# Feed-forward weights prepared in chunks inside the attention loop, and feed-forward tiles two deep

## The reference

```
q = layernorm(x) @ Wq;  k = ctx @ Wk;  v = ctx @ Wv        # 16 heads of 128
q, k = rmsnorm(q) * gq, rmsnorm(k) * gk                    # over the 128 of a head
x = x + tanh(g_xattn) * (softmax(q k^T / sqrt(128)) v) @ Wo

def weight_quant(w):                       # one scale for the whole matrix
    scale = max(mean(|w|), 1e-5);  return clip(round(w / scale), -1, 1) * scale
def act_quant(x):                          # one scale for each row
    scale = 127 / max(max|x|, 1e-5);  return clip(round(x * scale), -128, 127) / scale
def bitlinear(x, w): return act_quant(x) @ weight_quant(w)^T

n = layernorm(x)
x = x + tanh(g_ffn) * bitlinear(silu(bitlinear(n, w_gate)) * bitlinear(n, w_up), w_down)
```

## Time and profile before

| what | value |
|---|---|
| median of 3 runs (lowest, highest) | 2481.73 us (2481.36, 2483.34) |
| the profiled execution's own time | 2482.65 us |
| its span, first to last instruction | 2480.5 us, mean granted TensorE clock 0.97 |
| last product of attention, last residual | ends 2090.8 us, 2092.0 us |
| feed-forward block starts, first gate product | 2094.97 us, 2174.41 us |
| last store issued | 2478.1 us |

### The profile page before, as it was taken

One profiled execution on the slowest core, in us unless ns is written; L12 is line 12 of the kernel. 1 busy time (PEld: TensorE's weight loads), 2 busy tenths in 40 slices (PEclk: granted clock), 3 DMA queues, 4 the chain that ended last, 5 costly groups with the idle time before them and its releaser, 6 DMA issues. The chain is left out here.

```text
span 2480.5 us, 52473 instructions
## 1 busy us (share of the span) xinstructions
PE 2256.4 (91%) x16482; PEld 1597.2 (64%) x16634; DVE 1903.3 (77%) x4175; ACT 1577.8 (64%) x3226; POOL 1200.9 (48%) x1538
## 2 busy tenths in 40 slices
PE   2599999999999999999999999999999995589998
PEld 1377777777677767677767777777777773344443
DVE  4588878877878787877787788778887773589996
ACT  3567666766666666666666676667676763744443
POOL 4365646565656565656565656565656551000000
PEclk8799999999999999999999999999999998799999
DMA  6466666666666656666666666666666653434443
GB/s 199 103 112 113 122 111 119 113 121 112 116 116 121 107 118 116 122 112 116 114 122 113 116 112 123 113 115 113 124 113 118 115 113 106 160 77 106 118 114 93
DMA packets 887466, 289.31 MB, mean 117 GB/s; under 512 B 847760, under 2 KB 859312, under 8 KB 886704
## 3 DMA queue, kind: packets, MB, share of 16 engines
q1 hardware_dynamic: 887216, 286.15, 60.0%
HBM read 63.21 MB, written 13.11 MB: 31 GB/s over the span
## 5 line engine op out<-in xcount | busy, mean ns | idle before, releaser
L747 DVE TENSOR_TENSOR khat<-keys_ps,krs 128x512 f32<-128x512 f32 (+1 forms) x384 | 263.4, 686 | 289.9 <-POOL krs L989 289.9
L995 POOL TENSOR_TENSOR ksplit<-khat,ksplit 128x512 bf16<-128x512 f32 (+1 forms) x384 | 444.0, 1158 | 59.8 <-ACT ksplit L549 59.1
L986 POOL TENSOR_SCALAR kvar<-kss 128x4 f32<-128x4 f32 (+1 forms) x384 | 86.2, 225 | 674.0 <-DVE kss L737 674.0
L989 POOL TENSOR_TENSOR krs<-kvar,minus_half 128x4 f32<-128x4 f32 (+1 forms) x384 | 387.0, 1008 | 32.0
L569 ACT ACTIVATE early<-score_ps,nbias,qrs 100x361 f32<-100x361 f32 x512 | 330.5, 651 | 91.0 <-DVE nbias L765 88.5
L578 ACT ACTIVATE psplit<-early,rden 100x361 bf16<-100x361 f32 x512 | 304.9, 596 | 83.0 <-DVE rden L771 81.5
L554 ACT ACTIVATE ksq<-keys_ps 128x512 f32<-128x512 f32 (+1 forms) x384 | 228.6, 596 | 202.4 <-PE keys_ps L25 201.1
L777 DVE SCALAR_TENSOR_TENSOR psplit<-early,rden,psplit 100x361 bf16<-100x361 f32 x512 | 323.1, 641 | 7.8 <-ACT psplit L578 3.7
L549 ACT ACTIVATE ksplit<-khat 128x512 bf16<-128x512 f32 (+1 forms) x384 | 240.2, 625 | 115.5 <-DVE khat L747 105.0
L23 PE MATMUL keys_ps<-wk_hi,ctxT 128*128 128x512 bf16 (+1 forms) x649 | 249.8, 385 | 62.0 <-DVE khat L747 40.6
L755 DVE TENSOR_REDUCE nmax<-score_ps 100x1 f32<-100x361 f32 x512 | 269.1, 526 | 45.9 <-PE score_ps L25 45.9
(11 more groups left out here) (155 smaller groups left out, 5295.6 us busy)
## 6 DMA issues: line engine op xcount, KB each, us to landing
ctx_raw<-in_ctx SPq DMA_DIRECT2D x31, 256.0 KB, 3.0
xin<-in_x SPq DMA_DIRECT2D x32, 200.0 KB
xres<-in_x SPq DMA_DIRECT2D x32, 200.0 KB
x_rows<-xres SPq DMA_DIRECT2D x32, 200.0 KB
xin<-x_rows SPq DMA_DIRECT2D x25, 256.0 KB, 2.8
xres<-x_rows SPq DMA_DIRECT2D x25, 256.0 KB, 2.6
out<-xres SPq DMA_DIRECT2D x25, 256.0 KB, 2.9
kT<-ksplit SPq DMA_TRANSPOSE x384, 3.1
```

Of the source, the lines that this page charges most:

```text
L747: dve.tensor_tensor(khat[0:KV[t], k, :].rearrange("p (h d) -> p h d", h=G), keys_ps[k][0:KV[t], :].rearrange("p (h d) -> p h d", h=G), rs, ...
L989: pool.tensor_tensor(krs[0:KV[t], k, :], kvar[0:KV[t], k, :], minus_half[0:KV[t], 0:G], ALU.pow).then_inc(krs_done, 1)
L995: pool.tensor_tensor(ksplit[0:KV[t], t, 1, :], khat[0:KV[t], (u + t) % 2, :], ksplit[0:KV[t], t, 0, :], ALU.subtract).then_inc(k_lo_done, 1)
```

## The change

The host lays the three feed-forward weights out turned, as one array of 3 x 128 rows of 8192 f32 (w_ffn): row p of a matrix holds what partition p needs. A matrix is handled in 16 chunks of 512 columns, one in each of the 16 turns of a loop body. The loop of seven passes becomes: pairs 0 and 1 as straight code, a loop of three passes (one for each matrix) with a sum chunk in every turn, a loop of three passes with a chunk to be made ternary in every turn, and pairs 14 and 15 as before. In the first kind SP loads a chunk and ACT sums the absolute values; at the end of the pass DVE adds the 16 sums and SP stores them as a row of 128. In the second kind DVE first finds the scale from that row; each chunk is loaded again, scaled and rounded (one DVE instruction), clipped (a second), taken to bf16 by POOL and stored to DRAM (w_tern). In the last pair SP loads w_tern into the place of Wq's and Wk's parts, when these have been read for the last time. yT now shares its place with qsq.

The feed-forward block begins with x, reads only the stored sums, and runs two tiles deep: gate and up of tile t + 2 before down of tile t, statistics and quantising of x four tiles ahead. The quantised x goes through ACT's cast and a DMA transpose in place of PE's. The hidden rows are quantised by ACT in two halves and turned in two halves. A Silu at the start of the block comes before the tanh.

The attention part:

```diff
+    MATRICES, W_COLS = w_ffn.shape[0] // P, w_ffn.shape[1]
+    CHUNKS = BODY * UNITS
+    CHUNK = W_COLS // CHUNKS
+    SUM_LOOPS = (1, 1 + MATRICES)
+    TERN_LOOPS = (1 + MATRICES, 1 + 2 * MATRICES)
+    assert TERN_LOOPS[1] < PAIRS // BODY
...
+        w_raw, w_out = sb("w_raw", [P, CHUNK], F32), sb("w_out", [P, CHUNK], BF16)
+        w_abs, w_abs1 = sb("w_abs", [P, CHUNKS], F32), sb("w_abs1", [P, 1], F32)
+        w_part, w_tot = sb("w_part", [P, P], F32), sb("w_tot", [P, 1], F32)
+        w_scale, w_inv = sb("w_scale", [P, 1], F32), sb("w_inv", [P, 1], F32)
...
+            def load_chunk(j, i, u, k, job):
+                if job == "sum":
+                    sp.wait_ge(w_summed, chunk(i, u) + 1)
+                    sp.sem_inc(sp_passed, 1)
+                else:
+                    sp.wait_ge(w_rounded, tern_chunk(i, u) + 1)
+                    sp.sem_inc(sp_passed, 1)
+                sp.dma_start(w_raw[:, :], w_ffn[w_rows(j, job), k * CHUNK:(k + 1) * CHUNK]).then_inc(w_raw_in, 16)
+                if job == "tern" and k == 0:
+                    m = j - TERN_LOOPS[0]
+                    sp.wait_ge(w_inv_done, m + 1)
+                    sp.sem_inc(sp_passed, 1)
+                    sp.dma_start(w_part[:, :], w_sums[bass.ds(m, 1), :].partition_broadcast(P)).then_inc(w_part_in, 16)
+            def store_chunk(j, i, u, k, job):
+                if job == "tern":
+                    sp.wait_ge(w_rounded, tern_chunk(i, u) + 2)
+                    sp.sem_inc(sp_passed, 1)
+                    sp.dma_start(w_tern[w_rows(j, job), k * CHUNK:(k + 1) * CHUNK], w_out[:, :]).then_inc(w_tern_out, 16)
+                elif k == CHUNKS - 1:
+                    m = j - SUM_LOOPS[0]
+                    sp.wait_ge(w_abs_read, m + 2)
+                    sp.sem_inc(sp_passed, 1)
+                    sp.dma_start(w_sums[bass.ds(m, 1), :].rearrange("a p -> p a"), w_abs1[:, :]).then_inc(w_sums_out, 16)
+            def load_ternary(u):
+                gate_up = wq_split[:, :, :, :].rearrange("p a c n -> p a (c n)")
+                down = wk_split[:, :, :, :].rearrange("p a c n -> p (a c n)")
+                if u == 4:
+                    sp.wait_ge(w_tern_out, (MATRICES * CHUNKS + 1) * 16)
+                    sp.wait_ge(shared_done, use(PAIRS - 1, ("q", UNITS - 5, QD - 1))[0] + 1)
+                for m, part, parts in {4: ((0, 0, 4),), 5: ((0, 1, 4),), 6: ((0, 2, 4), (0, 3, 4), (1, 0, 4)),
+                                       7: ((1, 1, 4), (1, 2, 4), (1, 3, 4)), 8: ((2, 0, 2), (2, 1, 2))}.get(u, ()):
+                    if m == 2 and part == 0:
+                        sp.wait_ge(keys_done, tile(PAIRS - 1, UNITS - 1, KVT - 1) + 1)
+                    cols = slice(part * (W_COLS // parts), (part + 1) * (W_COLS // parts))
+                    dst = gate_up[:, m, cols] if m < 2 else down[:, cols]
+                    sp.dma_start(dst, w_tern[m * P:(m + 1) * P, cols]).then_inc(w_tern_in, 16)
...
+            def turn(i, u, last, par, j=None, job=None):
+                if job is not None:
+                    load_chunk(j, i, u, par * UNITS + u - 1, job)
...
+                    store_chunk(j, i, u, par * UNITS + u - 1, job)
+                if last:
+                    load_ternary(u)
...
+            for i in range(SUM_LOOPS[0] * BODY):
+                for u in range(1, UNITS + 1):
+                    turn(i, u, False, i % BODY)
+            with sp.Fori(*SUM_LOOPS) as j:
                 for r in range(BODY):
                     for u in range(1, UNITS + 1):
-                        turn(j * BODY + r, u, False, r)
-            for i in range(LOOPS * BODY, PAIRS):
+                        turn(j * BODY + r, u, False, r, j, "sum")
+            sp.wait_ge(w_sums_out, (MATRICES + 1) * 16)
+            sp.wait_ge(w_summed, MATRICES * CHUNKS + 1)
+            with sp.Fori(*TERN_LOOPS) as j:
+                for r in range(BODY):
+                    for u in range(1, UNITS + 1):
...
+            def sum_chunk(j, i, u, k):
+                eng.wait_ge(w_raw_in, (chunk(i, u) + 1) * 16)
+                if k == 0:
+                    eng.wait_ge(w_abs_read, j - SUM_LOOPS[0] + 1)
+                act.activation(w_raw[:, :], w_raw[:, :], ACT.Abs, accum_out=w_abs[:, k:k + 1]).then_inc(w_summed, 1)
...
+            def clip_chunk(j, i, u, k):
+                n = tern_chunk(i, u)
+                eng.wait_ge(w_raw_in, (chunk(i, u) + 1) * 16)
+                if k == 0:
+                    eng.wait_ge(w_inv_done, j - TERN_LOOPS[0] + 2)
+                dve.tensor_scalar(w_raw[:, :], w_raw[:, :], w_inv[:, 0:1], ROUND, ALU.mult, ALU.add).then_inc(w_scaled, 1)
+                eng.wait_ge(w_scaled, n + 1)
+                dve.tensor_scalar(w_raw[:, :], w_raw[:, :], ROUND + 1.0, ROUND - 1.0,
+                                  ALU.min, ALU.max).then_inc(w_clipped, 1)
...
+                    clip_chunk(j, i, u, par * UNITS + u - 1)
                     scale_keys(i, v + 2, 0)
...
                     scale_keys(i, v + 2, 1), scale_keys(i, v + 2, 2)
+                if job == "tern":
+                    clip_chunk(j, i, v, par * UNITS + v - 1)
...
+            def round_chunk(j, i, u, k):
+                n = tern_chunk(i, u)
+                eng.wait_ge(w_clipped, n + 1)
+                eng.sem_inc(pool_passed, 1)
+                eng.wait_ge(w_tern_out, n * 16 + 16)
+                eng.sem_inc(pool_passed, 1)
+                pool.tensor_scalar(w_out[:, :], w_raw[:, :], -ROUND, 1.0, ALU.add, ALU.mult).then_inc(w_rounded, 1)
...
                     query_scale(i, u)
+                if job == "tern":
+                    round_chunk(j, i, u, par * UNITS + u - 1)
                     key_scale(i, v + 2, 1), keys_lo(i, v + 2, 0)
...
                     keys_lo(i, v + 2, 1), keys_lo(i, v + 2, 2)
+                if job == "tern":
+                    round_chunk(j, i, v, par * UNITS + v - 1)
...
```

The feed-forward part (the steps of SP, PE, ACT and DVE) and the host's:

```diff
+            def step(t, s, ahead):
+                if ahead >= 5 or not isinstance(t, int):
+                    load_x(t + 5, 1 - s)
+                if ahead >= 1:
+                    turn_hidden(t + 1, 1 - s, 0)
+                if ahead >= 3:
+                    turn_x(t + 3, 1 - s)
+                if ahead >= 1:
+                    load_residual(t + 1, 1 - s)
+                    turn_hidden(t + 1, 1 - s, 1)
                 sp.wait_ge(res_done, t + 2)
                 sp.dma_start(out[bass.ds(t * P, P), :], xres[:, s, :]).then_inc(out_done[s], 16)
...
+            def step(t, s, ahead):
+                if ahead >= 2:
+                    gate_up(t + 2, s)
                 down(t, s)
...
+            def quantise(t, s, a):
+                cols = slice(a * HALF, (a + 1) * HALF)
+                eng.wait_ge(hinv_done, t + 1)
+                act.activation(hid[:, s, cols], hid[:, s, cols], ACT.Copy, bias=ROUND,
+                               scale=hinv[:, s:s + 1]).then_inc(hq_done, 1)
...
+            def step(t, s, ahead):
+                if ahead >= 2:
+                    gated(t + 2, s, 0)
+                if ahead >= 1:
+                    quantise(t + 1, 1 - s, 0)
+                if ahead >= 2:
+                    gated(t + 2, s, 1)
+                if ahead >= 1:
+                    cast_hidden(t + 1, 1 - s, 0)
+                if ahead >= 3:
+                    cast_x(t + 3, 1 - s)
+                if ahead >= 2:
+                    gated(t + 2, s, 2)
+                if ahead >= 1:
+                    quantise(t + 1, 1 - s, 1)
+                if ahead >= 2:
+                    gated(t + 2, s, 3)
+                if ahead >= 1:
+                    cast_hidden(t + 1, 1 - s, 1)
...
-                dve.tensor_scalar(hid[:, s, :], hid[:, s, :], hinv[:, 0:1], ROUND,
-                                  ALU.mult, ALU.add).then_inc(hq_done, 1)
...
+            def step(t, s, ahead):
+                if ahead >= 4:
+                    x_stats(t + 4, s)
+                down_scale(t, s)
+                if ahead >= 2:
+                    hidden(t + 2, s)
+                    hidden_scale(t + 2, s)
+                if ahead >= 4:
+                    x_quant(t + 4, s)
                 residual(t, s)
...
+    w = np.concatenate([inputs[n].T.reshape(-1, 128, inputs[n].shape[0]).transpose(1, 0, 2).reshape(128, -1)
+                        for n in _FFN])
```

More of the change, by code:

```diff
@@ L534, in _ @@
             first_turn(-1, UNITS)
-            with eng.Fori(0, LOOPS) as j:
-                for r in range(BODY):
-                    for u in range(1, UNITS, 2):
-                        two_turns(j * BODY + r, u, False, r)
-            for i in range(LOOPS * BODY, PAIRS):
+            for i in range(SUM_LOOPS[0] * BODY):
+                for u in range(1, UNITS, 2):
+                    two_turns(i, u, False, i % BODY)
+            for loops, job in ((SUM_LOOPS, "sum"), (TERN_LOOPS, "tern")):
+                with eng.Fori(*loops) as j:
+                    for r in range(BODY):
+                        for u in range(1, UNITS, 2):
```

(47 more changed lines are left out.)

382 lines of the change are left out of this document (173 added, 209 removed).

## The result

The changed kernel takes 2463.1 us (median of 4 runs, 2459.8 to 2469.8), the one before 2482.5 beside it: ratio 0.9925, 95% interval 0.9907 to 0.9944. The forecast was 2405.5 and the range ended at 2440. The sign was right, and most of the gain is missing: 19 us came, 76 were forecast. The profiled execution took 2469.8 us, the longest of the four; its span is 2468.0.

A forecast was written before the change was run, and what follows sets the result against it. PE was taken to bound the attention loop, with DVE and PE both nearly full in the feed-forward tiles. From 2482.65 us, -68 - 32 + 24 = -76 gave 2406.6, median 2405.5; range 2380 to 2440, own range 2390 to 2420.

The forecast's parts named there:

- Part 1, the hole: Feed-forward start: weight summing, rounding and transposes leave, so the first gate product comes some 11 us in: -68 us.
- part 2, the tiles: Feed-forward tiles: DVE loses work, PE becomes the bound at 10.4 us a tile instead of 11.67: -32 us.
- the DVE-bound rival: Feed-forward tiles stay DVE's, period 11.2 us, not 10.4: 18 us more, 2424 us; chance 0.12.
- Jumps back: Attention loop: four jumps at body ends instead of six, 3.1 us each: -6 us.
- Part 3, clips: Attention loop: DVE's clips delay PE, 28 us; even clips' delay taken as 1.8 us, bounds 1.0 (unblocked) and 2.6 (blocked).
- the 131 that the prediction named as a sign of being wrong: Attention loop: clip pairs forecast at 126 to 129 us; under 124 or over 131 would show the prediction wrong.
- price for all clips (57 us): Rival: POOL and DVE block each other at even turns' clips, 57 us for 28, time 2435; chance 0.22.
- Rounding: Attention loop: POOL's rounding, near 0.75 us, goes into an engine idling 40%: nothing, at most 10 us.
- Sums on ACT: Attention loop, pairs 2 to 7: 48 sums at 0.2 us a pair, with weight_sum and weight_scale 2 us in all.
- Chunk loads: Attention loop: loads behind pT's transposes in SP's queue land 0.7 us before use in even turns: nothing.
- the slower rival: Attention loop: chunk loads come late, ACT or DVE stands still and PE after it; time 2521 us; chance 0.04.
- with weight_sum and weight_scale 2 us in all: Attention loop: the sums on ACT plus the closing sum and scale steps together cost 2 us.

The follow-up runs named there:

- e4: Changed kernel without the loop's chunk loads, sums, scales, clips and rounding, stores of constants kept: 2381.6 us, ratio 0.9596.
- e3: Changed kernel with both moves: sums' store behind x1 stores and residual loads, DVE's scale just before its first clip: 2440.2 us.
- e10: As e3, with the 96 clip instructions left out: 2417.2 us, ratio 0.972.
- e7: As e3, with POOL's rounding cut to 2 of 512 columns: 2440.5 us, ratio 0.9824.
- e8: As e3, with ACT's sum of a chunk cut to 2 of 512 columns: 2438.9 us, ratio 0.9813.
- e18: As e13, without clips and without chunk loads, sums kept whole: 2394.4 us, ratio 0.9639.
- e15: As e13, without chunk loads, clips and all but 2 columns of the sums: 2387.7 us, ratio 0.9606.
- e12: As e3, with the 96 chunk loads left out, all instructions and stores kept: 2436.4 us, ratio 0.9813.
- e17: As e13, with the chunk loads left out: 2422.8 us, ratio 0.9751.
- e13: As e3, with the sums turned on DVE and stored as 4 pieces of 128 bytes, the quick store: 2426.6 us, ratio 0.9772.
- e2: Changed kernel with DVE's three scale instructions moved from the clip body's first group to just before its first clip: 2447.6 us, ratio 0.9854.
- e5: As e3, with the context load of the next pair's first batch issued ahead of the x1 stores: 2435.1 us, ratio 0.9801.
- e14: As e13, with the context load ahead of the x1 stores, scaling on ACT and clipping on POOL instead of DVE: 2406.1 us, ratio 0.9679.

## Why the prediction was wrong

The measured time is 57.6 us over the forecast: 52 in the chunk work, priced at 30, and 6 in the rest. By the ratios, times 2482.5 us, the chunk work costs 82 us, and in this order the two moves give back 25 of it, the quick store 13 more, and clips with loads and sums 41; 2.5 are left.

- **Part 1, the hole (-68) and part 2, the tiles (-32): right.** First gate product 10.9 us after the block's start (11 predicted), 273.0 us from it to the end (306.1 before, less 32: 274), of these 257.3 to the end of the last up product (257.7 forecast, though the products in that sum come to 248.9 and not to 249.2). A tile takes 10.36 us: PE's down products start at 2224.21 here and at 2234.57 in the next tile; PE waits for DVE only 4.1 us in two places of the window, so the DVE-bound rival is out.
- **Jumps back (-6): wrong.** Without chunk work the forecast is 2375.7, and e4 measures 2381.6. There the feed-forward block begins at 2094.24, and at 2094.97 before: the attention loop is not 6 us shorter. The term took each jump at 3.1 us whatever the loop; e4's four cost 4.0 to 4.7 each, as much as the six before. Why a jump costs more there is open.
- **Part 3, clips (28): right in size, in part by luck.** 26 us (e3 to e10), if clips are taken away alone. By the forecast each even clip delays by 1.8 us; one of the four in a pair takes 2.3 and the others 1.0 to 1.2, but for one of 1.9. The first groups inside a body lose 2.2 to 3.3 us, where 1.9 (1.5 and 0.4) were priced, and the rest less than priced. Clip pairs last 128.6 to 129.8 us, at and over the upper end of the forecast's 126 to 129, but those with a body's end in them 141.1 and 140.2, beyond the 131 that the prediction named as a sign of being wrong. Both ends of the bound are seen side by side: 0.43 us and 1.80 us for the same instruction. Only one even clip of each pair, in the first group, meets a whole ksplit; no instruction of the others takes over 0.77 us, but for one of 1.36. Where a clip is blocked only its second instruction is, so it takes 2.3 us and not 2.6. The Trainium skill, page "SBUF — State Buffer", section "SBUF: two separate sides", has DVE and GpSimd take a shared port pair as an exclusive lock, for a whole instruction. The trace agrees for one SBUF operand as well, by the 1.80 and 1.37 us. As a price for all clips (57 us) it was wrong, since timing decides which of them meet ksplit.
- **Rounding (0): nothing against it**, by e7. **Sums on ACT (2): right or some 6 us short**; e8 has 2.5 and e18 to e15 has 8.
- **Chunk loads (0): short by 2.5 to 5 us, or right**, since 0 is inside the intervals of e12 and e17. ACT waits 8.6 us in all for the 48 it sums, DVE 0.5 for the 48 it clips: the slower rival did not happen.
- **The failed step: "with weight_sum and weight_scale 2 us in all".** I priced these two by their instructions (0.2 and 0.6 us) and left out what goes with them: a store and a load on SP, and a DVE wait for the load. In their place the runs show 38 us (e3 and e13), most of the 52 by which the 30 for chunk work was short. The store of 128 pieces of 4 bytes has no row before, and I gave it no bound. It lands after 7.3 to 11.3 us, and x1's store and what stands behind it wait with it at three loop ends. The load of the sums is issued behind x1's store, the residual loads and a chunk load, and DVE waits for it in order ahead of khat: 22.9 us of DVE in three places. Moving it (e2) gave 15.5 us. Both are visible in the diff: the one stands in SP's order ahead of the x1 stores, the other ahead of khat on DVE.
- **The rest of the 52:** loads and sums, up to 11 us over their price, with 2.5 us of rounding, the small sum steps and SP's waits. Within intervals of 7 to 10 us more cannot be told apart.

The clock is a part of it. PE's idle stretches at the loop ends are followed by a lower grant, as in e5:

```profile
1138.00:1140.00 2.00, 1.99 (x23) 1.75 (x22) 0.56 (x3) 1.20 (x4) 1.08 (x2) 1.00 0.41 55
1140.00:1142.00 2.00, 0.00 (x0) 0.00 (x0) 0.00 (x0) 0.00 (x0) 0.00 (x0) 0.73 0.75 171
1142.00:1144.00 2.00, 0.00 (x0) 0.00 (x0) 0.52 (x3) 0.00 (x0) 0.00 (x0) 0.50 1.01 217
1144.00:1146.00 2.00, 0.20 (x2) 0.19 (x3) 1.93 (x7) 0.16 (x1) 0.18 (x1) 0.50 1.24 121
```

At full speed while PE was busy, it is at the lower level (0.50, 1.2 GHz) once PE has stood still, and PE starts again at that level. The rows behind them:

```profile
1146.00:1151.00 5.00, 5.00 (x21) 3.37 (x20) 3.24 (x7) 2.29 (x5) 4.75 (x6) 0.50 0.89 183
1152.00:1155.00 3.00, 3.00 (x34) 2.81 (x33) 2.09 (x6) 2.22 (x6) 1.29 (x4) 1.00 0.47 96
```

PE works 5 us at half speed before it is back at full speed, so this wait of about 6 us costs some 2.5 us beyond its own length (an estimate from these rows: half of the busy time at 0.50).

## What to carry to other kernels

Price the bookkeeping of a change as closely as its bulk: 144 instructions of DVE and ACT and 96 loads cost 41 us here, three stores of half a kilobyte and three loads of 64 KB, with the waits for them, 38. Look at the shape of a small transfer (how many pieces, of how many bytes), at what stands behind it in the queue, and put a wait for memory on an in-order engine where nothing urgent follows. When a cost is tested by shrinking an instruction, look in the trace whether it did shrink: one that waits for another engine's instruction keeps its time.

## What the hardware showed that I had not expected

- A store of 128 pieces of 4 bytes to memory lands after 7.3 to 11.3 us, of 64 bytes after 2.0 to 3.0, and in e5 transfers issued behind the first, of 64 and 256 KB, land 10 to 11 us after their issue. Loads of 4-byte pieces at the kernel's start, with nothing ahead of them, are no such case: g_row's 512 bytes land after 2.0 us.
- The block works both ways: POOL's small ln_rstd, 0.57 us by its median, takes 1.26 in the first group of each of the six clip pairs, with a clip beside it (at 1845.80 us, for one; the clip's first instruction starts 0.35 us later and is not held), and never over 0.72 in e4, without clips.
- Where DVE turns the sums (e13, e14, e15), its work at the end of the first sum body is followed by 4.8 to 5.2 us in which it waits for nothing that the profile shows (the jump back), where PE's own take 2.6 to 3.4 in e13 and e14. Without the turning it comes to the same point and waits for ACT there, 3.15 us after its last work in e3. e13's line, then e3's:

```profile
618.43 0.69 DVE L856 TENSOR_REDUCE kss<-ksq 128x4 f32<-128x512 f32 x1 [5.17 <-issue]
```

```profile
617.30 0.69 DVE L854 TENSOR_REDUCE kss<-ksq 128x4 f32<-128x512 f32 x1 [3.15 <-ACT ksq L654]
```

In e14 PE then waits 2.8 us for khat. The fourth groups ahead of the first two sum ends last 37 to 38 us in e14 and e15, 33 to 34 in e3 and before, so some of the quick store's gain is lost there. These runs suggest that the turning instruction makes DVE's jump longer; none of them shows it, since no run has it elsewhere.
